# An attention and feed-forward block on one core: a planner that works in rounds, with measured durations, on four buffers of P, and TensorE summing only the last whole blocks

## The reference, cut to what matters

```python
x = L0_attn_x                                # (4, 2048, 512) f32, 16 heads of 32
x = x + LN(attn(LN(x)))                      # attn: q, k, v, p are x @ W + b, all 512 x 512
x = x + LN(ffn(LN(x)))                       # ffn: x @ W[idx] + b[idx], idx = argmax(logits + gumbel)
# inside attn
att = einsum('bhtd,bhsd->bhts', q, k) / sqrt(32)
att = where(causal and s % 4 != 3, att, -inf)    # every fourth key is never seen
y = einsum('bhts,bhsd->bhtd', softmax(att), v)
```

## Time and profile before

| | before |
|---|---|
| median of 3 runs | 2530.27 us (2527.24 to 2530.47) |
| the profiled execution's own time | 2530.78 us |
| its span, first to last instruction | 2529.0 us |
| TensorE busy | 2397.7 us (95%) |
| VectorE busy | 1780.0 us (70%) |
| ScalarE busy | 1486.3 us (59%) |
| GpSimd busy | 1430.0 us (57%) |
| mean granted TensorE clock | 0.983 |

### The profile page before, as it was taken

How to read it: one execution, slowest core, us unless ns; L and a number is a source line. 1 busy time by engine, 2 the same in 40 slices (tenths; PEclk the granted TensorE clock), 3 DMA queues, 4 the chain that set the end, 5 groups by cost and what they waited for, 6 DMA issues and landing times.

```text
span 2529.0 us, 43113 instructions
## 1 busy us (share of the span) xinstructions
PE 2397.7 (95%) x15380; PEld 937.7 (37%) x15380; DVE 1780.0 (70%) x4820; ACT 1486.3 (59%) x2654; POOL 1430.0 (57%) x1318
## 2 busy tenths in 40 slices
PE   4899999999999999999999999999999999999997
PEld 2343333333344433333344443333334443333322
DVE  8777677777387777677457867767738677767764
ACT  5545566565655556556655565656665565665663
POOL 2345465675656466476763637557756455656633
PEclk9899999999999999999999999999999999999988
DMA  7213030111133213021122303102114130301001
GB/s 187 67 48 86 22 86 22 35 51 40 47 94 69 60 41 71 18 57 46 32 64 77 92 26 80 38 23 61 36 28 103 45 93 23 87 23 37 24 1 33
DMA packets 224352, 137.46 MB, mean 54 GB/s; under 512 B 146730, under 2 KB 196618, under 8 KB 224138
## 3 DMA queue, kind: packets, MB, share of 16 engines
q1 hardware_dynamic: 222310, 134.65, 20.9%
q10 hardware_dynamic: 1828, 0.07, 0.0%
HBM read 39.69 MB, written 16.78 MB: 22 GB/s over the span
## 4 chain that ended last, share of the span: by engine, by line
PE 60%; DVE 18%; POOL 8%; ACT 5%; issue 5%; DMA 3%; SPq 1%; ACTq 0%; POOLq 0%; DVEq 0%
PE acc L1200 12%; PE acc L1164 9%; PE acc L1184 9%; PE acc L1215 7%; PE acc L1135 7%; PE acc L1136 7%; PE acc L1137 7%; ACT P L845 4%; DVE MP L943 4%; POOL P L721 4%; DVE acc L939 3%; DVE STA L911 2%; DMA XB<-in_L_attn_x_dram 2%; POOL XP L707 1%; PE acc L1188 1%
## 5 line engine op out<-in xcount | busy, mean ns | idle before, releaser
L845 ACT ACTIVATE P<-acc,EX 128x512 f32<-128x512 f32 (+2 forms) x1920 | 1065.1, 638 | 339.5 <-PE acc L1188 182.5
L943 DVE TENSOR_REDUCE MP<-acc 128x1 f32<-128x512 f32 (+1 forms) x1088 | 720.2, 679 | 251.7 <-PE acc L1164 248.7
L721 POOL TENSOR_TENSOR P<-P 128x512 f32<-128x512 f32 x546 | 686.3, 1287 | 96.6 <-ACT P L845 96.3
L1164 PE MATMUL acc<-KST,QST 96*128 96x512 f16 (+10 forms) x2112 | 575.1, 336 | 29.1 <-DVE MP L943 13.1
L939 DVE CUSTOM_DVE_ANT_0 acc<-acc,CB 128x96 f32<-128x96 f32 (+7 forms) x1024 | 449.6, 454 | 192.2 <-PE acc L1164 190.7
L1184 PE MATMUL acc<-QST,KST 98*128 98x512 f16 (+2 forms) x1920 | 555.7, 358 | 19.6 <-DMA QST<-MROW 8.4
L1200 PE MATMUL acc<-P,V 128*32 128x512 f32 (+2 forms) x3840 | 465.6, 557 | 22.5 <-ACT P L845 13.6
L1164 PEld LDWEIGHTS acc<-KST,QST 96*128 96x128 f16 x2112 | 193.0, 98 | 360.1 <-issue 112.0
L726 POOL TENSOR_TENSOR SC<-SC 128x512 f32<-128x512 f32 x64 | 81.3, 1271 | 432.6 <-DVE SC L977 432.5
L1184 PEld LDWEIGHTS acc<-QST,KST 98*128 98x128 f16 x1920 | 179.5, 98 | 376.5 <-issue 147.0
L1215 PE MATMUL acc<-P,ONES 128*32 128x512 f32 (+2 forms) x2688 | 290.4, 516 | 0.7 <-POOL P L721 0.7
(11 more groups left out here) (140 smaller groups left out, 2812.5 us busy)
## 6 DMA issues: line engine op xcount, KB each, us to landing
QST<-QKH SPq DMA_DIRECT2D x128, 128.0 KB, 3.2
XR<-in_L_attn_x_dram SPq DMA_DIRECT2D x60, 256.0 KB, 2.8
out_dram<-XR SPq DMA_DIRECT2D x60, 256.0 KB, 2.1
KST<-QKH SPq DMA_DIRECT2D x128, 96.0 KB, 2.6
XB<-in_L_attn_x_dram SPq DMA_DIRECT2D x48, 252.0 KB
QST<-QKL SPq DMA_DIRECT2D x64, 128.0 KB, 3.3
KST<-QKL SPq DMA_DIRECT2D x64, 96.0 KB, 2.7
XB<-in_L_attn_x_dram SPq DMA_DIRECT2D x20, 256.0 KB, 3.5
```

Of the source, the lines that this page charges most:

```text
L721: e.tensor_tensor(P[:, acc, a, :], P[:, acc, a, :], P[:, buf, a, :], ALU.add).then_inc(g_s, 1)
L845: e.activation(P[:, p_buf[u, g, sb_], a, t0:512], bank(*step)[:, t0:512], ACT.Exp, scale=EX[:, 1:2]).then_inc(a_e, 1)
L943: e.tensor_reduce(maxima(u, g)[:, r, a, ci:ci + 1], bank(*s)[:, 0:n], AX.X, ALU.max).then_inc(v_m, 1)
L1164: i = e.matmul(bank(*s)[:, 0:n], QST[0:96, h, 128 * r:128 * r + 128], KST[0:96, h, c0:c0 + n], start=True, stop=True)
```

## The change

- **Rounds.** `run` now takes its ranks from `self.rank`. After the first plan, `backwards` plays the program from its end: each step becomes ready when all its users are placed, resources are taken by the step that gives them back, and among ready steps the one with the latest end in the last plan goes first. A step can't be placed more than WINDOW = 45000 ns ahead of its place in the last plan. The start times so found, negated, are the next ranks. Up to 5 rounds, and the shortest plan of the six is taken.
- **Durations.** `norm` 455 to 750 ns, `high` 270/340 to 400/470, `peak` on VectorE 75 + n (+ 40) to 72 + 1.04n.
- **on_pe.** TensorE itself sums the blocks from 3j - max(j - 1, 0) on. The others, 1 to 2, 1 to 4 and 1 to 6 for j = 1, 2, 3, are added (before: 2; 2, 3, 5; 2, 3, 5, 6, 8).
- **P** has 4 buffers in one ring: block 0 keeps its buffer for the phase, the other three rotate.
- **V** holds 4 units' blocks instead of 5, **YX** 3 tiles instead of 4 (the last tile of all uses XR), and small constants have moved from V to YX. So `evac` of v, from unit 4 on, waits for a `pv` of the last unit of the batch before instead of one two units back, and `evac` of p waits for `add_y` three tiles back.

```diff
 def on_pe(j, sb):
-    return sb >= 3 * j or sb % 3 == 1
+    return sb >= 3 * j - max(j - 1, 0)
...
-    last, acc = 2, 0
+    ring = [0, 1, 2, 3]
     for u in range(NB * NJ):
         for g in range(4):
-            new = [i for i in range(3) if i not in (acc, last)][0]
-            ring = [last, acc]
-            acc = first[u, g] = new
             for sb in range(3 * (u % NJ) + 3):
-                last = acc if sb == 0 else ring[(sb - 1) % 2]
...
+                now = buf[u, g, sb] = ring.pop(0)
+                if sb:
+                    ring.append(now)
+                else:
+                    first[u, g] = now
...
+            ring.append(first[u, g])
...
+    SWITCH = 100
+    ROUNDS, WINDOW = 5, 45000
...
+        self.rank = {key: step[0] for key, step in self.steps.items()}
+        plans = [self.run()]
+        for _ in range(self.ROUNDS):
+            self.rank = self.backwards()
+            if self.rank is None:
+                break
+            plans.append(self.run())
+        _, lists, self.bank, self.emptier, self.times = min(plans, key=lambda plan: plan[0])
...
-            add("dve", at - 1, 455, ("norm", 0, u, r), [("gp", "rstd", 0, u, r)])
+            add("dve", at - 1, 750, ("norm", 0, u, r), [("gp", "rstd", 0, u, r)])
...
-                add("dve", at, 270 if which == "k" else 340, ("high", job), [("act", "evac", job)], [("QKH", ("sp", "spread", job))])
+                add("dve", at, 400 if which == "k" else 470, ("high", job), [("act", "evac", job)], [("QKH", ("sp", "spread", job))])
...
-                add("dve", at, 75 + n + 40 * end, ("peak", u, g, r, a, ci), [("pe", "peak", u, g, r, a, ci)]
+                add("dve", at, 72 + 1.04 * n, ("peak", u, g, r, a, ci), [("pe", "peak", u, g, r, a, ci)]
...
-                         + ([("gp", "add_y", u - 1, r)] if u else []))
+                         + ([("sp", "store", *divmod(n - 6, 4))] if n == 4 * self.NU - 1 else
+                            [("gp", "add_y", *divmod(n - 3, 4))] if n > 2 else []))
...
+    def backwards(self):
...
+        length = max(end for _, end in self.times.values())
+        late = {key: length - end for key, (_, end) in self.times.items()}
...
+        def offer(key):
+            if late[key] - self.WINDOW > now:
+                events.append((late[key] - self.WINDOW, "offer", key))
+                return
+            ready[key[0]].append((late[key], key))
+            ready[key[0]].sort(key=lambda x: x[0])
...
+        return {key: -at for key, at in starts.items()} if len(starts) == len(self.steps) else None
...
-        V = sb("V", [128, 3 * (NJ + 1), 512], F32)
+        V = sb("V", [128, 3 * NJ, 512], F32)
-        P = sb("P", [128, 3, 4, 512], F32)
+        P = sb("P", [128, 4, 4, 512], F32)
-        YX = sb("YX", [128, 4, 512], F32)
+        YX = sb("YX", [128, 3, 512], F32)
...
-                        if u > 1:
-                            ac.wait_ge(p_pv, PE["pv", u - 2, 3, 3 * ((u - 2) % NJ) + 2])
+                        if u >= NJ:
+                            ac.wait_ge(p_pv, PE["pv", u // NJ * NJ - 1, 3, 3 * (u % NJ) + 2])
```

More of the change, by code:

```diff
@@ L294, in run @@
     def run(self):
[L295 to L302, removed]
+        left = {key: len(set(step[2])) for key, step in self.steps.items()}
+        lists = {e: [] for e in self.ENGINES}
         ready = {e: [] for e in lists}
@@ L362, in run @@
                     if not left[y]:
-                        ready[y[0]].append((self.steps[y][0], y))
+                        ready[y[0]].append((self.rank[y], y))
                         ready[y[0]].sort(key=lambda z: z[0])
         assert len(through) == len(self.steps)
+        self.times = times
+        return max(end for _, end in times.values()), lists, bank, emptier, times
+    def backwards(self):
+        length = max(end for _, end in self.times.values())
+        late = {key: length - end for key, (_, end) in self.times.items()}
+        left = {key: len(users) for key, users in self.users.items()}
+        taken = {}
+        for key, step in self.steps.items():
+            for t, until in step[3]:
+                taken.setdefault(until, []).append(t)
+        most = {**self.MOST, **self.TURNS}
+        used, banks = {t: 0 for t in most}, 0
+        ready, free, events, now = {e: [] for e in self.ENGINES}, {e: True for e in self.ENGINES}, [], 0
+        starts, tiled = {}, False
+        def offer(key):
[4 more added lines that the diff above has]
+            ready[key[0]].sort(key=lambda x: x[0])
+        for key, n in left.items():
+            if not n:
+                offer(key)
+        while True:
+            for e in self.ENGINES:
+                if not free[e]:
+                    continue
+                for at, (_, key) in sorted(enumerate(ready[e]),
+                                           key=lambda x: e == "pe" and tiled and x[1][1][1] not in ("pv", "sum")):
+                    takes = taken.get(key, ())
+                    if all(used[t] < most[t] and (t not in self.MOST or banks < self.BANKS) for t in takes):
+                        del ready[e][at]
+                        for t in takes:
+                            used[t] += 1
+                            banks += t in self.MOST
+                        ns = self.steps[key][1]
+                        if e == "pe" and tiled != (key[1] in ("pv", "sum")):
+                            ns += self.SWITCH
+                            tiled = not tiled
+                        free[e] = False
+                        starts[key] = now + ns
+                        events.append((now + ns, "free", key))
+                        for n in set(self.steps[key][2]):
+                            events.append((now + ns + (self.LAG[n[0]] if n[0] != e else 0), "used", n))
+                        for t, until in self.steps[key][3]:
+                            events.append((now + ns + self.LAG[until[0]], "empty", t))
+                        break
+            if not events:
+                break
+            now = min(at for at, _, _ in events)
+            due = [x[1:] for x in events if x[0] <= now]
+            events = [x for x in events if x[0] > now]
+            for kind, x in due:
+                if kind == "free":
+                    free[x[0]] = True
+                elif kind == "offer":
+                    offer(x)
+                elif kind == "used":
+                    left[x] -= 1
+                    if not left[x]:
+                        offer(x)
+                else:
+                    used[x] -= 1
+                    banks -= x in self.MOST
+        return {key: -at for key, at in starts.items()} if len(starts) == len(self.steps) else None
```

85 lines of the change are left out of this document (47 added, 38 removed).

## The result

| | before | after |
|---|---|---|
| median | 2530.37 us (2527.24 to 2532.96) | 2467.12 us (2459.62 to 2473.42) |
| ratio | | 0.9749, 95% interval 0.9717 to 0.9782 |
| the profiled execution's own time | 2530.78 us | 2459.62 us |
| its span | 2529.0 us | 2457.7 us |
| mean granted TensorE clock | 0.983 | 0.974 |

The change makes the kernel 63 us faster, 2.5%. Forecast were 132, and 2467 lies just above the range's upper end of 2462. The profiled execution is the fastest of the four; numbers from its trace stand against 2459.6.

What follows compares the result with a forecast made beforehand. TensorE, busy for 2397.7 of 2529.0 us, was taken to bound the kernel. The terms summed as 2530.8 - 41.3 - 45.8 - 45 = 2398.7, so 2399 us, 5.2% faster, with a range of 2350 to 2462.

Steps and rivals of the forecast that it cites:

- TensorE bounds, and how its time is made up: TensorE busy 2397.7 of 2529.0 us; a tiled block costs 0.86 us, an excursion into the tiled form 0.235.
- 48 sums less, -41.3 us: TensorE sums 288 blocks instead of 336, each 0.86 us, all of it on TensorE.
- 195 excursions less, -45.8 us: TensorE's order has 578 changes of form instead of 968; each excursion saved is 0.235 us.
- Waits, -45 us: TensorE's mid-kernel idle time (63.1 us) and some 75 us of unseen waits, 138 in all; a third was taken.
- GpSimd costed at 0: 186 more additions on GpSimd, +239 us to 1669, taken as covered by TensorE; upper bound all 239 on the path.
- VectorE's norms, 13 us, covered: 256 VectorE norms wait beside GpSimd's additions as the mean one does, 1.23 times as often: 13 us, covered.
- The Trainium skill's rule on shared ports: VectorE in a two-port mode and GpSimd exclude each other for a whole instruction; it speaks against the change.
- case B: The rest of the chain does not shorten; only TensorE's 60% share of the removed work counts: 2479 us, chance 0.10.
- A: Only TensorE's work goes, the waits stay: 2444 us, chance 0.25.
- C: GpSimd's additions become the path at blocks 1 to 6 (j = 3) and 1 to 4 (j = 2): 2566 us, chance 0.03.
- V, YX, start, `scale`: Smaller V and YX, later expert choice at the start, `scale` behind the additions: 0 each, up to +5 each.
- Signs given: Trace after: TensorE idle under 2% per stretch from 200 us, waits on ScalarE's P under 8 us, norms near 0.8.

Runs made afterwards that it cites:

- the gap: Changed kernel with GpSimd waiting for its own last addition ahead of each block's first, so at every fourth addition: 2402.51 us, 0.9487.
- old sums: Changed kernel with the old rule on_pe (336 sums on TensorE, 546 additions on GpSimd): 2428.65 us; with a wait ahead of each block's first addition, 2406.23 us.
- the spread blocks: Changed kernel with as many sums and additions, but TensorE's own blocks every third one instead of the last whole ones: 2405.16 us, 0.95.

## Why the prediction was wrong, step by step

- *TensorE bounds, and how its time is made up:* right. The medians of lone blocks, pairs and triples in the trace of after are again 1.00, 1.86 and 2.72 us. Groups of three blocks are 48 (44 before), and some 75 are longer, where before none was.
- *48 sums less, -41.3 us; 195 excursions less, -45.8 us:* right as TensorE's work: busy time fell by 101.7 to 2296.0, inside the 2280 to 2310 given, and L1308 has 2304 rows. As time of the kernel the first term failed. With the gap the swap brings 4 us where the terms make 31; without it, it costs 38.
- *Waits, -45 us:* the waits that were counted did go. With old sums and the gap, the time is 124 us under before, of which 240 excursions are 56; 68 are left for waits and clock, half of the 138 and not a third. These 68 are what is left over, not measured by themselves. In the changed kernel itself, 2530.8 - 87.1 = 2443.7 is left after the two sure terms and 2459.6 was measured: waits and clock together cost 16 us more than before.
- *GpSimd costed at 0:* busy 1656.6 for 1670 given. Its two effects were named and missized. The pace: `exp` waits for it 30.8 us (6.1 before). It may be the 19 us between the spread blocks and the changed ones, both with gap; no run shows it by itself. The other effect is the next point.
- *VectorE's norms, 13 us, covered:* **this is the step that failed.** The forecast read one norm of 1.26 us beside one addition, took the mean of all norms and scaled it by GpSimd's busy share. That mean hid one norm of 5.36 us, the same thing in the trace of before:

```profile
603.53 5.36 DVE L922 TENSOR_SCALAR XB<-XB,MV,RR 128x512 f32<-128x512 f32 x1
```

  The step that matters was another (MHL<-MX), the wait is no share of an addition but can last for many of them, and it isn't covered, as every peak stands behind it. VectorE's busy time rose by 129 us instead of 17, of which the norms are 24 and MHL<-MX 56. With the long steps undone by gaps, 65 us come back, and the kernel is at 2402.5 where 2399 was forecast. The agreement is partly luck: the sums were worth less and the waits more.
- *The Trainium skill's rule on shared ports* (page "SBUF — State Buffer", section "Who interferes with whom") was put down as a reason for case B. VectorE was indeed kept waiting beside GpSimd, but for up to 11.75 us, where the rule speaks of one whole instruction and an addition is 1.29. That a shared port is what they collided on, no run here shows by itself.
- *Cases:* A (2444) and B (2479) had 0.35 together, and the result lies between them. B's own mechanism, VectorE held up by GpSimd, was at work, without B's reasoning by shares of the chain; its price of one addition for each norm was wrong as well. C's place was right (blocks 1 to 6), its size far off.
- *V, YX, start, `scale`:* 0 each is in line with the trace, 34.0 and 13.4 us idle at the start for 33.2 and 10.3. None was tried alone.
- *Signs given:* waits for P under 8 us, yes for `pv` (3.3), no over all of TensorE's lines (9.8). Idle time under 2% of each stretch, no: 10% from 1000 to 1200. Norms near 0.8 us in the mean, 0.83 to 0.90. The sign of being wrong did show: waits of `exp` for GpSimd's P at 30.8 us, with idle TensorE beside them.

What stays open: why a VectorE step waits for one addition at most early in a busy stretch of GpSimd and for many late in it, why only some of the late ones do, and why short gaps end it even where long mixed stretches remain. Which resource it is was not shown by itself; a form free of it was not found for this step.

## What to carry to other kernels

Look in the trace for the longest run of GpSimd instructions without a gap, not only at its busy share, and for VectorE steps whose longest duration is far from their median. A wait of 0.17 us on its own last instruction, every eight, cost nothing here and brought 73 us. Work taken from the bounding engine counts only as far as the engine that takes it leaves everyone's buffers and turns where they were: where the additions stood was worth more than how many there were. And when TensorE stops for several us, add the time at the lower clock behind it.

## What the runs showed of the hardware that was not expected

- A VectorE step of 0.17 us can last 11.75 us beside back-to-back additions on GpSimd (12.61 with the spread blocks). This was seen for tensor_scalar, cast and scalar_tensor_tensor with inputs in SBUF, not for reductions from PSUM, which ran at 0.68 us in the mean before and after.
- No step of these kinds of over 2.2 us began less than 12 us into GpSimd's unbroken stretch, in eight traces without a gap. With a gap after every 8 additions, 9.88 us, there was none.
- With a gap of 0.17 us between additions, at each, every fourth or every eighth, no step of these kinds was over 1.9 us, in any of the eight versions that have it.
- 7.4 idle us of 12 were followed by 4 us at a granted clock of 0.50.
